# Sharing each K/V weight slab between two token groups in a fused attention and feed-forward layer

## The chip, the cores and the metric

The kernel runs on the 8 cores of one Trainium2 chip. All eight run the same program on their own inputs, with no exchange between them. The metric is the device time of the slowest core in microseconds (us).

## What is computed

One layer on an input of 2 batches x 4096 tokens x 4096 features, in float32 outside and bfloat16 inside the kernel. The reference, cut to what matters:

```python
def attn(q, w_qkv, w_dense):          # q: [2, 4096, 4096]
    qkv = q @ w_qkv.T                 # 32 query heads, 8 K and 8 V heads of 128
    ...
    scores = einsum('bskgd,btkd->bkgst', qh, kh) * scale   # causal
    probs = softmax(where(causal, scores, min))
    return einsum('bkgst,btkd->bskgd', probs, vh).reshape(...) @ w_dense.T

def ffn(x, w12, b12, w3, b3):
    x1, x2 = split(x @ w12.T + b12)   # 4096 each
    return (silu(x1) * x2) @ w3.T + b3

x = x + layernorm(attn(layernorm(x)))
x = x + layernorm(ffn(layernorm(x)))
```

## The kernel before

A core owns 8 blocks of 128 tokens of one batch, for which it computes the output, and it computes K and V for all 32 blocks of that batch itself. Weights come as a tape of slabs in the order of use: a slab holds the 4096 x 128 weights of one output chunk, in float32 in memory (2 MB), cast to bfloat16 while it is loaded.

The program goes through these stages:

1. **K and V (loop over `grp`, 8 groups of 4 blocks).** `prep_block` (four times per group) loads a block (`xscr<-xb`, L304), takes the layernorm statistics on DVE (L218, L223) and ACT (L227, L231), normalizes (L239), and transposes the block in four batches of eight 128 x 128 transposes on PE (L248), each copied out by DVE (L253) into one of the two slots of `xnT2`. Then come 16 output chunks, 8 of K and 8 of V. A chunk is `proj_ochunk`: 32 matmuls of 128 x 512 (L281), which consume one slab. ACT evicts the chunk into `kstage` (L335) or `vstage` (L344). A K chunk is stored at once. A V chunk is transposed on PE right behind its own matmuls (L248, four transposes that wait for ACT's eviction), copied by DVE into `vtstage` and stored.
2. **Q.** Eight `prep_block` for the core's own blocks fill both slots of `xnT2`; then 32 slabs, each used for both slots (`gi` 0 and 1): 64 chunks, evicted by ACT into `qstage` (L377).
3. **Attention**, then the output projection (`pp<-attn`), then the residual, two layernorms and the transposes into `xn2T` for the 8 own blocks (loop over `tb`).
4. **Feed-forward.** 32 times: a slab for `x1` and one for `x2` on both halves of the tokens (`th`, 512 tokens each), SiLU and product; then `w3`, the last layernorm and the store.

The order on every engine is the order in which the code emits operations: each of the five engines replays its own list. So the preparation of a group stands on PE and DVE behind all chunks of the group before it, the V transposes included.

**The slab ring.** `wsl` has 3 slots, each for half a slab (`load_half`, issued by POOL at L204). Half n goes into slot n % 3 and waits until the last matmul that reads half n-3 is done:

```python
    def load_half():
        n = half_loaded[0]
        slot = n % 3
        waits = [half_done[n - 3]] if (n - 3) in half_done else []
```

`half_done` is written by `proj_ochunk`, so where a slab is used by two calls, the second call sets it. In stages 2 to 4 a slab serves two calls; in stage 1 it serves one. The whole K/V weight set therefore stands 8 times on the tape. The loads of the next group's blocks stand in POOL's list behind all half-slab loads of this group.

Of the kernel before, what the change touches and what calls it, by code (L numbers as in the profile page):

```python
# [12 lines left out]
AF = mybir.ActivationFunctionType  # L13
# [21 lines left out]
TB = 128  # L35
GA1 = 4
EXP_SHIFT = -25.0

def derived(cfg):
    d = dict(cfg)  # L40
    d["D"] = cfg["IC"] * 128
    d["S"] = cfg["NBLK"] * TB
    d["TPC"] = cfg["NOWN"] * TB
    d["M"] = cfg["MC"] * 128
    d["QOC"] = cfg["KVH"] * cfg["G"]
    assert d["QOC"] == cfg["IC"]
    d["KVOC"] = 2 * cfg["KVH"]
    d["NG1"] = cfg["NBLK"] // GA1
    d["OWNG"] = cfg["NOWN"] // 2
    d["NA2T"] = d["OWNG"] * TB  # L50
    assert d["NA2T"] <= 512
    d["NSLAB_A1"] = d["NG1"] * d["KVOC"]
    d["NSLAB"] = (d["NSLAB_A1"] + d["QOC"] + cfg["IC"] + 2 * cfg["MC"] + cfg["IC"])
    pads = []
    for m in range(cfg["NOWN"] // 2):
        pads.append(2 * R * m + R)
        pads.append(2 * R * m + 2 * R)
    d["PADS"] = pads
    return d
# [45 lines left out]
def build(cfg):  # L105
    d = derived(cfg)
    IC, KVH, G, NBLK, NOWN, MC = (cfg[k] for k in ("IC", "KVH", "G", "NBLK", "NOWN", "MC"))
    D, S, TPC, M, QOC, KVOC = (d[k] for k in ("D", "S", "TPC", "M", "QOC", "KVOC"))
# [182 lines left out]
    def sdma(sem, dst_ap, src_ap, waits):  # L291
        p.op("sync", lambda sy, dst_ap=dst_ap, src_ap=src_ap: sy.dma_start(dst_ap, src_ap),
             waits=waits, inc=sem, incn=16)
        return (sem, p.v(sem))
# [22 lines left out]
        return ev  # L317

    pb = 0
    for grp in range(NG1):  # L320
        evs = []
        for j in range(GA1):
            blk = grp * GA1 + j
            evs.append(prep_block(xbt[blk], pb % 2, grp % 2, j * 128,
                                  is_first=(grp == 0 and j == 0)))
            pb += 1
        xn_ok = ("vEV", evs[-1])
        for o in range(KVOC):
# [5 lines left out]
            if o < KVH:
                p.op("scalar", lambda s, bank=bank, par=par: s.activation(  # L335
                    kstage[:, par, :], pp[:, bank, :], AF.Copy),
                    waits=[("mPE", mm), WAR.get(("kst", par), ("aR", 0))], inc="aEV")
                bank_free[bank] = ("aEV", p.v("aEV"))
                sv = sdma(f"dSK{par}", KDR[o][:, grp * 512:(grp + 1) * 512],
                          kstage[:, par, :], [("aEV", p.v("aEV"))])  # L340
                WAR[("kst", par)] = sv
            else:
                kv = o - KVH
                p.op("scalar", lambda s, bank=bank, par=par: s.activation(  # L344
                    vstage[:, par, :], pp[:, bank, :], AF.Copy),
                    waits=[("mPE", mm), WAR.get(("vst", par), ("mTR", 0))], inc="aEV")
                bank_free[bank] = ("aEV", p.v("aEV"))
                aev = p.v("aEV")
                ev = transpose_batch(
                    lambda j, par=par: vstage[:, par, 128 * j:128 * (j + 1)],  # L350
                    4, vtstage[:, par, :, :],
                    first_waits=[("aEV", aev)],
                    dst_war=[WAR.get(("vts", par), ("aR", 0))])
                WAR[("vst", par)] = ("mTR", p.v("mTR"))
                sv = sdma(f"dSV{par}",
                          VDR[kv, grp * GA1:(grp + 1) * GA1].rearrange("b t d -> t b d"),
                          vtstage[:, par, :, :], [("vEV", ev)])
                WAR[("vts", par)] = sv
        WAR[("xnT", grp % 2)] = ("mPE", p.v("mPE"))

    A1_K = [("dSK0", p.v("dSK0")), ("dSK1", p.v("dSK1"))]
    A1_V = [("dSV0", p.v("dSV0")), ("dSV1", p.v("dSV1"))]
# [163 lines left out]
    C_MM = p.v("mPE")  # L526
    C_EV = p.v("vEV")

    for tb in range(NOWN):
        par = tb % 2  # L530
        w0 = [("mPE", C_MM)] if tb < 2 else [WAR.get(("xstr", par), ("vLN", 0))]
        p.op("gpsimd", lambda g, tb=tb, par=par: g.dma_start(xstrip[:, par, :], xow[tb]),
             waits=w0, inc=f"dX{par}", incn=16)
        dx = (f"dX{par}", p.v(f"dX{par}"))
        ar = ln_stats(ytm[:, tb, :], par, first_waits=[("vEV", C_EV)])
        x2w = WAR.get(("x2s", par), ("aR", 0))
        p.op("vector", lambda v, tb=tb, par=par: v.tensor_scalar(
            x2stage[:, par, :], ytm[:, tb, :], mvt[:, par, 0:1], rst[:, par, 0:1],
            ALU.subtract, ALU.mult),
            waits=[("aR", ar), x2w] + ([("mTR", A_TR_DONE)] if tb < 2 else []), inc="vLN")  # L540
        vv = p.v("vLN")
        p.op("vector", lambda v, par=par: v.tensor_tensor(
            x2stage[:, par, :], x2stage[:, par, :], xstrip[:, par, :], ALU.add),
            waits=[("vLN", vv), dx], inc="vLN")
        vv2 = p.v("vLN")
        sv = sdma(f"dSX{par}", X2DR[tb], x2stage[:, par, :], [("vLN", vv2)])
        WAR[("x2s", par)] = sv
        ar3 = ln_stats(x2stage[:, par, :], par, first_waits=[("vLN", vv2)])
        nv = ln_norm(xstrip[:, par, :], x2stage[:, par, :], par, ar3)
        dst_war = ([("mIT", B_IT), ("vAT", B_AT), ("vMS", B_MS)] if tb == 0 else ())  # L550
        transpose_strip(
            xstrip[:, par, :], IC,
            lambda ic0, n, tb=tb: xn2T[:, ic0:ic0 + n, tb * 128:(tb + 1) * 128],
            src_ready=("vLN", nv), dst_war=dst_war)
        WAR[("xstr", par)] = ("mTR", p.v("mTR"))
    XN2T_OK = ("vEV", p.v("vEV"))
    X2_ST = [("dSX0", p.v("dSX0")), ("dSX1", p.v("dSX1"))]

    for m in range(MC):
        h1 = load_slab()  # L560
        mm1 = {}
        mm2 = {}
        for th in range(NTH):
            extra = [XN2T_OK] if (m == 0 and th == 0) else []
            mm1[th] = proj_ochunk(th % 2, lambda i, th=th: xn2T[:, i, th * THW:(th + 1) * THW],
                                  h1, extra=extra, nw=THW)
        h2 = load_slab()
        for th in range(NTH):
            mm2[th] = proj_ochunk(2 + th % 2, lambda i, th=th: xn2T[:, i, th * THW:(th + 1) * THW],
                                  h2, nw=THW)  # L570
        for th in range(NTH):
            par = th % 2
            p.op("scalar", lambda s, th=th, par=par, m=m: s.activation(  # L573
                silst[:, par, 0:THW], pp[:, th % 2, 0:THW], AF.Silu, bias=bsb[:, m:m + 1]),
                waits=[("mPE", mm1[th]), WAR.get(("sil", par), ("vLN", 0))], inc="aEV")
            bank_free[th % 2] = ("aEV", p.v("aEV"))
            aev = p.v("aEV")
            x4w = ([("mPE", C_MM), ("mTR", p.v("mTR"))] + X2_ST) if (m == 0 and th == 0) else []
            p.op("vector", lambda v, th=th, par=par, m=m: v.scalar_tensor_tensor(  # L579
                x4[:, m, th * THW:(th + 1) * THW], pp[:, 2 + th % 2, 0:THW], bsb[:, MC + m:MC + m + 1],  # L580
                silst[:, par, 0:THW], ALU.add, ALU.mult),
                waits=[("mPE", mm2[th]), ("aEV", aev)] + x4w, inc="vLN")
            bank_free[2 + th % 2] = ("vLN", p.v("vLN"))
            WAR[("sil", par)] = ("vLN", p.v("vLN"))
# [77 lines left out]
def make_tape(cfg, w_qkv, w_dense, w12, w3):  # L662
    d = derived(cfg)
    IC, KVH, MC = cfg["IC"], cfg["KVH"], cfg["MC"]
    D, M = d["D"], d["M"]

    def slabs(W):
        O = W.shape[0]
        W4 = W.reshape(O // 128, 128, IC, 128)
        return np.ascontiguousarray(W4.transpose(0, 3, 2, 1))  # L670

    wq = w_qkv[0:D]
    wk = w_qkv[D:D + KVH * 128]
    wv = w_qkv[D + KVH * 128:D + 2 * KVH * 128]
    kv_slabs = np.concatenate([slabs(wk), slabs(wv)], axis=0)
    s1 = slabs(w12[0:M])
    s2 = slabs(w12[M:2 * M])
    inter = np.empty((2 * MC, 128, IC, 128), dtype=w12.dtype)
    inter[0::2] = s1
    inter[1::2] = s2  # L680
    tape = np.concatenate([np.concatenate([kv_slabs] * d["NG1"], axis=0),
                           slabs(wq), slabs(w_dense), inter, slabs(w3)], axis=0)
    assert tape.shape[0] == d["NSLAB"]
    return np.ascontiguousarray(tape)
# [75 lines left out]
```

How the kernel before makes its waits and increments, by code:

```python
    def replay(self, eng, obj):  # L90
        for fn, waits, inc, incn in self.ops[eng]:
            for s, v in waits:
                obj.wait_ge(self.sems[s], v)
            ins = fn(obj)
            if inc is not None:
                ins.then_inc(self.sems[inc], incn)
```

## Time and profile before

| | |
|---|---|
| time of the two runs shown | 5386.72 and 5641.98 us, median 5514.35 us |
| the profiled execution: its own time | 5381.83 us |
| its span, slowest core | 5380.3 us |
| spans of the eight cores | 5357.6 to 5380.3 us |
| mean granted TensorE clock, each core | 0.908 to 0.910 |
| half-slab loads | 576 of 512 KB (as bfloat16) |
| HBM read | 771.87 MB |

The profile is of one execution on its slowest core. "Granted clock" is the share of TensorE's full clock (2.4 GHz) that the chip let through. Busy time of an engine is summed over its instructions; idle time is put down to what ended it. A PE row's duration of one matmul (about 380 ns) is longer than the distance between two, since matmuls are pipelined; the distances are read from start times.

### The profile page before, as it was taken

How to read it: one execution, taken by the hardware profiler on the slowest of the kernel's cores; microseconds unless marked ns; L12 is line 12 of the kernel's file. 1: busy time of each engine (PE TensorE's matmuls, PEld its weight loads, DVE VectorE, ACT ScalarE, POOL GpSimd, SP SyncE). 2: the span in 40 equal slices, each digit the busy share in tenths (PEclk: the TensorE clock that was granted, in tenths of full speed). 3: DMA queues.
4: the chain of work that ended last, by engine and by line, in shares of the span. 5: the costliest groups of instructions: out<-in, count | busy, mean ns of one | idle time of the engine just before them, and what ended most of it. 6: DMA issues, size and time to landing. Idle time of an engine off the chain costs nothing.

```text
span 5380.3 us, 55151 instructions; the slowest of 8 cores (5357.6 to 5380.3 us)
## 1 busy us (share of the span) xinstructions
PE 4209.1 (78%) x20096; PEld 1903.7 (35%) x20096; DVE 1144.8 (21%) x1552; ACT 975.8 (18%) x1603; POOL 331.3 (6%) x631
## 2 busy tenths in 40 slices
PE   5586587678666998888888888871699999988880
PEld 2233233333233443333333333331344444433330
DVE  2202211221223000443333300016300000011116
ACT  0000000000000000778888600000000000000000
POOL 0010011011000000000000000000000000000000
PEclk9797798788787999999999999995799999999995
DMA  6786686686673555222222133343344444433334
GB/s 100 117 139 108 103 147 114 107 142 115 107 121 71 94 96 114 65 65 60 74 62 58 33 64 65 65 71 78 75 79 75 75 79 77 72 63 63 63 59 187
DMA packets 222943, 473.46 MB, mean 88 GB/s; under 512 B 81328, under 2 KB 138672, under 8 KB 212448
## 3 DMA queue, kind: packets, MB, share of 16 engines
q0 software_dynamic: 89952, 352.48, 40.1%
q1 hardware_dynamic: 132736, 117.46, 7.3%
q8 instruction: 175, 2.87, 0.2%
q14 instruction: 80, 0.66, 0.1%
HBM read 771.87 MB, written 50.33 MB: 153 GB/s over the span
## 4 chain that ended last, share of the span: by engine, by line
PE 63%; DVE 13%; ACT 10%; DMA 7%; issue 6%; ACTq 0%; DVEq 0%; SPq 0%; POOL 0%; POOLq 0%
PE pp L281 54%; ACT psl L417 8%; DVE stats L218 5%; PE pt L248 5%; DMA wsl<-wtape 4%; PE pp L465 2%; DVE xnT L253 2%; DMA xscr<-xb 1%; PE pp L471 1%; DMA xstrip<-X2DR 1%; PE pp L409 1%; DVE xnscr L239 1%; DVE psl L456 1%; DVE lntmp L481 1%; DVE ydst L595 1%
## 5 line engine op out<-in xcount | busy, mean ns | idle before, releaser
L281 PE MATMUL pp<-xnT,wsl 128*128 128x512 bf16 x6144 | 1367.1, 382 | 39.3 <-DMA wsl<-wtape 23.0
L281 PE MATMUL pp<-xn2T,wsl 128*128 128x512 bf16 x4096 | 887.7, 380 | 3.0 <-DMA wsl<-wtape 2.0
L281 PEld LDWEIGHTS pp<-xnT,wsl 128*128 128x128 bf16 x6144 | 594.1, 98 | 791.2 <-issue 111.9
L417 ACT ACTIVATE psl<-pp,bsb 128x512 bf16<-128x512 f32 x1152 | 743.3, 687 | 194.0 <-PE pp L409 190.4
L281 PEld LDWEIGHTS pp<-xn2T,wsl 128*128 128x128 bf16 x4096 | 401.4, 98 | 489.2 <-issue 8.3
L204 POOL DMA_DIRECT2D wsl<-wtape x576 | 304.1, 529 | 4350.3 <-PE pp L281 4301.6
L465 PE MATMUL pp<-psl,vsl 128*128 128x512 bf16 x1152 | 442.6, 384 | 125.4 <-DVE psl L456 79.8
L248 PE MATMUL pt<-idsb,xnscr 128*128 128x128 bf16 x1280 | 162.0, 307 | 479.0 <-DVE xnscr L239 363.6
L281 PE MATMUL pp<-attn,wsl 128*128 128x512 bf16 x2048 | 454.5, 380 | 4.9 <-DVE attn L486 4.5
L281 PE MATMUL pp<-x,wsl 128*128 128x512 bf16 x2048 | 452.3, 379 | 1.1 <-DVE x L579 1.1
L471 PE MATMUL pp<-psl,onesb 128*128 128x512 bf16 x1152 | 443.4, 385 | 0.0
L409 PE MATMUL pp<-qsl,ksl 128*128 128x512 bf16 x1152 | 418.8, 382 | 14.6 <-DMA qsl<-QDR 14.6
L456 DVE TENSOR_TENSOR psl<-psl,msl 128x512 bf16<-128x512 bf16 x256 | 107.1, 424 | 960.3 <-ACT psl L417 494.5
L248 PEld LDWEIGHTS pt<-idsb,xnscr 128*128 128x128 bf16 x1280 | 124.0, 139 | 515.9 <-issue 515.9
L281 PEld LDWEIGHTS pp<-attn,wsl 128*128 128x128 bf16 x2048 | 196.3, 98 | 233.8 <-issue 8.6
L281 PEld LDWEIGHTS pp<-x,wsl 128*128 128x128 bf16 x2048 | 195.7, 98 | 228.7 <-issue 1.5
L465 PEld LDWEIGHTS pp<-psl,vsl 128*128 128x128 bf16 x1152 | 111.2, 97 | 386.6 <-issue 373.6
L253 DVE COPY vtstage<-pt 128x512 bf16<-128x512 bf16 x64 | 27.2, 425 | 1014.8 <-PE pt L248 1014.8
L481 DVE RECIPROCAL lntmp<-pp 128x512 f32<-128x512 f32 x64 | 214.9, 3358 | 60.8 <-PE pp L471 60.8
L579 DVE SCALAR_TENSOR_TENSOR x<-pp,bsb,silst 128x512 bf16<-128x512 f32 x64 | 48.1, 751 | 842.8 <-PE pp L281 842.8
L218 DVE BATCH_NORM_STATS2 stats<-xscr 128x6 f32<-128x512 bf16 x320 | 193.4, 677 | 21.1 <-DMA xscr<-xb 21.1
L573 ACT ACTIVATE silst<-pp,bsb 128x512 bf16<-128x512 f32 x64 | 44.0, 687 | 822.9 <-PE pp L281 822.9
(40 smaller groups left out, 1178.0 us busy)
## 6 DMA issues: line engine op xcount, KB each, us to landing
wsl<-wtape POOLq DMA_DIRECT2D x576, 512.0 KB, 6.0
xscr<-xb POOLq DMA_DIRECT2D x32, 1024.0 KB, 10.7
msl<-mtab SPq DMA_DIRECT2D x64, 512.0 KB, 3.6
yout<-ostage SPq DMA_DIRECT2D x8, 2048.0 KB, 7.9
KDR<-kstage SPq DMA_DIRECT2D x64, 128.0 KB, 6.7
VDR<-vtstage SPq DMA_DIRECT2D x64, 128.0 KB, 5.9
xscr<-xown POOLq DMA_DIRECT2D x8, 1024.0 KB, 8.0
QDR<-qstage SPq DMA_DIRECT2D x64, 128.0 KB, 4.5
```

The lines of the kernel that those rows point to most:

```text
L204: p.op("gpsimd", lambda g, n=n, slot=slot: g.dma_start(wsl[:, slot, :, :], wtape[n // 2][:, (n % 2) * IC2:(n % 2 + 1) * IC2, :]), waits=wa ...
L218: p.op("vector", lambda v, k=k, par=par, in_ap=in_ap: v.bn_stats(stats[:, par, 6 * k:6 * k + 6], in_ap[:, 512 * k:512 * (k + 1)]), waits=( ...
L239: p.op("vector", lambda v, out_ap=out_ap, in_ap=in_ap, par=par: v.tensor_scalar(out_ap, in_ap, mvt[:, par, 0:1], rst[:, par, 0:1], ALU.sub ...
L248: p.op("tensor", lambda t, j=j, tiles_fn=tiles_fn: t.transpose(pt[:, j, :], tiles_fn(j), idsb), waits=(list(first_waits) + [pt_free[0]] if ...
L253: p.op("vector", lambda v, dst_ap=dst_ap, n=n: v.tensor_copy(dst_ap, pt[:, 0:n, :]), waits=[("mTR", tr)] + list(dst_war), inc="vEV")
L281: p.op("tensor", lambda t, i=i, bank=bank, hs=hs, rhs_fn=rhs_fn, nw=nw: t.matmul(pp[:, bank, 0:nw], wsl[:, hs, i % IC2, :], rhs_fn(i), sta ...
L409: p.op("tensor", lambda t_, sbank=sbank, slot=slot, qslot=qslot, tt=t: t_.matmul(pp[:, sbank, :], ksl[:, slot, tt, :], qsl[:, qslot].rearr ...
L417: p.op("scalar", lambda s, sbank=sbank, sl3=i % 3: s.activation(psl[:, sl3, :], pp[:, sbank, :], AF.Exp, bias=bsb[:, SHIFT_COL:SHIFT_COL + ...
L456: p.op("vector", lambda v, sl3=sl3, qslot=qslot, w=w: v.tensor_tensor(psl[:, sl3, :], psl[:, sl3, :], msl[:, qslot, w, :], ALU.mult), wait ...
L465: st=(t == 0), sp=(t == pad - 1): t_.matmul(pp[:, pb, :], vsl[:, slot, tt, :], psl[:, sl3, :], start=st, stop=sp, skip_group_check=True),
L471: st=(t == 0), sp=(t == pad - 1): t_.matmul(pp[:, ob, :], onesb, psl[:, sl3, :], start=st, stop=sp, skip_group_check=True),
L481: p.op("vector", lambda v, par=par: v.reciprocal(lntmp[:, par, :], pp[:, ONB[par], :]), waits=[("mIT", itv), lnt_war[par]], inc="vAT")
```

## The change

The loop over 8 groups becomes a loop over 4 pairs of groups. A pair first prepares its 8 blocks, 4 into each slot of `xnT2`; then every K/V slab is loaded once and used for both groups (`gi` 0 and 1). The tape holds the K/V weights 4 times. The PSUM bank of a chunk is now `(2 * o + gi) % 4` and the staging buffer is `gi`; both still alternate from chunk to chunk as before. Both slots of `xnT2` are free for the next pair once the last matmul of the pair is done.

In the feed-forward stage the first matmul no longer waits for the transposes of all own blocks, but for those of its own half of the tokens; the first matmul of the other half has a wait of its own.

```diff
-    d["NSLAB_A1"] = d["NG1"] * d["KVOC"]
+    d["NSLAB_A1"] = (d["NG1"] // 2) * d["KVOC"]
...
-    for grp in range(NG1):
-        evs = []
-        for j in range(GA1):
-            blk = grp * GA1 + j
-            evs.append(prep_block(xbt[blk], pb % 2, grp % 2, j * 128,
-                                  is_first=(grp == 0 and j == 0)))
-            pb += 1
-        xn_ok = ("vEV", evs[-1])
+    for pair in range(NG1 // 2):
+        xn_ok = {}
+        for gi in range(2):
+            grp = 2 * pair + gi
+            evs = []
+            for j in range(GA1):
+                blk = grp * GA1 + j
+                evs.append(prep_block(xbt[blk], pb % 2, gi, j * 128,
+                                      is_first=(pair == 0 and gi == 0 and j == 0)))
+                pb += 1
+            xn_ok[gi] = ("vEV", evs[-1])
         for o in range(KVOC):
             halves = load_slab()
-            bank = o % 4
-            mm = proj_ochunk(bank, lambda i, g2=grp % 2: xnT2[:, g2, i, 0:512],
-                             halves, extra=[xn_ok], nw=512)
-            par = (grp * KVOC + o) % 2
...
+            for gi in range(2):
+                grp = 2 * pair + gi
+                bank = (2 * o + gi) % 4
+                mm = proj_ochunk(bank, lambda i, gi=gi: xnT2[:, gi, i, 0:512],
+                                 halves, extra=[xn_ok[gi]], nw=512)
+                par = gi
...
-        WAR[("xnT", grp % 2)] = ("mPE", p.v("mPE"))
+        WAR[("xnT", 0)] = ("mPE", p.v("mPE"))
+        WAR[("xnT", 1)] = ("mPE", p.v("mPE"))
...
+        th_of = (tb + 1) * TB // THW - 1 if ((tb + 1) * TB) % THW == 0 else None
+        if th_of is not None:
+            XN2T_TH[th_of] = ("vEV", p.v("vEV"))
...
-            extra = [XN2T_OK] if (m == 0 and th == 0) else []
+            extra = [XN2T_TH[th]] if m == 0 else []
...
-    tape = np.concatenate([np.concatenate([kv_slabs] * d["NG1"], axis=0),
+    tape = np.concatenate([np.concatenate([kv_slabs] * (d["NG1"] // 2), axis=0),
```

The body of the chunk (eviction, V transposes, stores) is the same, one level deeper.

On POOL, from the program's start, the loads of blocks (`xscr`) and of half slabs (`wsl`) change so:

```order
-L304 DMA xscr<-xb 128x4096 x4
+L304 DMA xscr<-xb 128x4096 x8
 L204 DMA wsl<-wtape 128x2048 x32
-L304 DMA xscr<-xb 128x4096 x4
+L304 DMA xscr<-xb 128x4096 x8
 L204 DMA wsl<-wtape 128x2048 x32
```

Each run of 32 half slabs now serves 8 blocks of tokens, and there are 4 such runs where there were 8.

On PE, where a group ends and the next begins, before: the last V chunk (32 matmuls) and its transposes (`vstage`), the 128 transposes of the next group's preparation (`xnscr`), its 8 K chunks and first V chunk in a row (288 matmuls), and the first V transposes.

```order
L281 MATMUL pp<-xnT_50,wsl 128x512 x32
L248 MATMUL pt<-idsb,vstage 128x128 x4
L248 MATMUL pt<-idsb,xnscr 128x128 x128
L281 MATMUL pp<-xnT_50,wsl 128x512 x288
L248 MATMUL pt<-idsb,vstage 128x128 x4
```

The same place after, between the first pair and the second:

```order
L281 MATMUL pp<-xnT_50,wsl 128x512 x32
L248 MATMUL pt<-idsb,vstage 128x128 x4
L248 MATMUL pt<-idsb,xnscr 128x128 x256
L281 MATMUL pp<-xnT_50,wsl 128x512 x544
L248 MATMUL pt<-idsb,vstage 128x128 x4
```

The preparation is now of 8 blocks, and 544 matmuls (16 K chunks and the first V chunk) follow it; there are 4 such places with the Q stage's where there were 8, and the V transposes keep their place behind each V chunk.

At the start of the feed-forward stage on PE (`xstrip` are the transposes of the last own block; `vEV` counts DVE's copies out of the transposes, `dW` the slab loads), before:

```order
L248 MATMUL pt<-idsb,xstrip 128x128 x7
L281 MATMUL pp<-xn2T,wsl 128x512 [waits dW0,aEV,vEV]
L281 MATMUL pp<-xn2T,wsl 128x512 x15
L281 MATMUL pp<-xn2T,wsl 128x512 [waits dW1]
L281 MATMUL pp<-xn2T,wsl 128x512 x15
L281 MATMUL pp<-xn2T,wsl 128x512 [waits dW0,aEV]
```

And after:

```order
L248 MATMUL pt<-idsb,xstrip 128x128 x7
L281 MATMUL pp<-xn2T,wsl 128x512 [waits dW1,aEV,vEV]
L281 MATMUL pp<-xn2T,wsl 128x512 x15
L281 MATMUL pp<-xn2T,wsl 128x512 [waits dW2]
L281 MATMUL pp<-xn2T,wsl 128x512 x15
L281 MATMUL pp<-xn2T,wsl 128x512 [waits dW1,aEV,vEV]
```

The first feed-forward matmul still stands behind all transposes of all 8 own blocks in PE's list. What changed is the count of `vEV` that it waits for, the added wait of the other half of the tokens, and the ring slots (the number of half slabs before this stage has changed).

## Rows read from the trace of the kernel before

**Rows 1.** page: granted clock in 40 slices, chain that ended last

```profile
PEclk9797798788787999999999999995799999999995
...
PE 63%; DVE 13%; ACT 10%; DMA 7%; issue 6%; ACTq 0%; DVEq 0%; SPq 0%; POOL 0%; POOLq 0%
PE pp L281 54%; ACT psl L417 8%; DVE stats L218 5%; PE pt L248 5%; DMA wsl<-wtape 4%; PE pp L465 2%; DVE xnT L253 2%; DMA xscr<-xb 1%; PE pp L471 1%; DMA xstrip<-X2DR 1%; PE pp L409 1%; DVE xnscr L239 1%; DVE psl L456 1%; DVE lntmp L481 1%; DVE ydst L595 1%
```

**Rows 2.** timeline of ACT: start us, us, op; evictions of projected chunks

```profile
88.32 0.60 ACT L335 ACTIVATE kstage<-pp 128x512 bf16<-128x512 f32 x1 [18.46 <-PE pp L281]
95.23 0.60 ACT L335 ACTIVATE kstage<-pp 128x512 bf16<-128x512 f32 x1 [6.31 <-PE pp L281]
...
147.58 0.60 ACT L344 ACTIVATE vstage<-pp 128x512 bf16<-128x512 f32 x1 [6.90 <-PE pp L281]
...
197.98 0.60 ACT L344 ACTIVATE vstage<-pp 128x512 bf16<-128x512 f32 x1 [7.81 <-PE pp L281]
206.38 0.60 ACT L344 ACTIVATE vstage<-pp 128x512 bf16<-128x512 f32 x1 [7.81 <-PE pp L281]
279.62 0.60 ACT L335 ACTIVATE kstage<-pp 128x512 bf16<-128x512 f32 x1 [18.24 <-PE pp L281]
...
398.62 0.60 ACT L344 ACTIVATE vstage<-pp 128x512 bf16<-128x512 f32 x1 [7.97 <-PE pp L281]
473.74 0.60 ACT L335 ACTIVATE kstage<-pp 128x512 bf16<-128x512 f32 x1 [18.75 <-PE pp L281]
...
1438.66 0.60 ACT L335 ACTIVATE kstage<-pp 128x512 bf16<-128x512 f32 x1 [19.78 <-PE pp L281]
...
1499.53 0.60 ACT L344 ACTIVATE vstage<-pp 128x512 bf16<-128x512 f32 x1 [6.52 <-PE pp L281]
...
1559.08 0.60 ACT L344 ACTIVATE vstage<-pp 128x512 bf16<-128x512 f32 x1 [7.96 <-PE pp L281]
1695.10 0.60 ACT L377 ACTIVATE qstage<-pp 128x512 bf16<-128x512 f32 x1 [19.38 <-PE pp L281]
...
1806.92 0.60 ACT L377 ACTIVATE qstage<-pp 128x512 bf16<-128x512 f32 x1 [6.31 <-PE pp L281]
```

**Rows 3.** windows: K chunks, preparation of four blocks, Q, feed-forward

```profile
core 0: us, PE busy (x) PEld busy (x) DVE busy (x) ACT busy (x) POOL busy (x), PEclk, DMA share, GB/s
79.60:148.40 68.80, 64.81 (x288) 27.97 (x288) 0.00 (x0) 5.38 (x9) 9.35 (x18) 1.00 0.87 141
...
209.00:271.00 62.00, 16.21 (x129) 12.44 (x130) 37.03 (x56) 1.99 (x8) 2.64 (x5) 0.50 0.45 77
...
1685.50:1807.00 121.50, 120.53 (x546) 53.88 (x547) 0.00 (x0) 9.63 (x17) 8.45 (x16) 0.98 0.48 87
...
3821.00:4712.00 891.00, 887.87 (x4099) 401.48 (x4098) 48.07 (x64) 45.28 (x65) 67.54 (x128) 1.00 0.45 75
```

**Rows 4.** line L281 in 80:1560: what its matmuls waited for

```profile
  DMA wsl<-wtape: 19.5, 36
...
  ACT kstage L335: 4.5, 5
```

**Rows 5.** line L281 in 1685:2141 (Q)

```profile
  DMA wsl<-wtape: 3.5, 4
```

**Rows 6.** timeline, end of first group, and of the last

```profile
195.43 1.07 POOL L304 DMA_DIRECT2D xscr<-xb  x2
...
209.03 4.85 DVE L218 BATCH_NORM_STATS2 stats<-xscr 128x6 f32<-128x512 bf16 x8 [0.81 <-DMA xscr<-xb]
...
1560.83 4.84 DVE L218 BATCH_NORM_STATS2 stats<-xscr 128x6 f32<-128x512 bf16 x8
```

**Rows 7.** slab issues of 80:148, then of 1685:1807: count, KB, us to landing

```profile
wsl<-wtape POOLq DMA_DIRECT2D x17, 512.0 KB, 6.5
...
wsl<-wtape POOLq DMA_DIRECT2D x16, 512.0 KB, 6.3
```

**Rows 8.** timeline, start of the feed-forward matmuls

```profile
3820.66 19.59 PE L281 MATMUL pp<-xn2T,wsl 128*128 128x512 bf16 x83 [0.94 <-DVE xn2T L253]
```

More of the change, by code:

```diff
@@ L319, in build @@
     pb = 0
-    for grp in range(NG1):
-        evs = []
-        for j in range(GA1):
-            blk = grp * GA1 + j
-            evs.append(prep_block(xbt[blk], pb % 2, grp % 2, j * 128,
-                                  is_first=(grp == 0 and j == 0)))
-            pb += 1
-        xn_ok = ("vEV", evs[-1])
+    assert NG1 % 2 == 0
+    for pair in range(NG1 // 2):
[9 more added lines that the diff above has]
+            xn_ok[gi] = ("vEV", evs[-1])
@@ L328, in build @@
         for o in range(KVOC):
             halves = load_slab()
-            bank = o % 4
-            mm = proj_ochunk(bank, lambda i, g2=grp % 2: xnT2[:, g2, i, 0:512],
-                             halves, extra=[xn_ok], nw=512)
-            par = (grp * KVOC + o) % 2
[L334 to L358, printed above, removed]
@@ L359, in build @@
-        WAR[("xnT", grp % 2)] = ("mPE", p.v("mPE"))
+            for gi in range(2):
[4 more added lines that the diff above has]
+                par = gi
+                if o < KVH:
+                    p.op("scalar", lambda s, bank=bank, par=par: s.activation(
+                        kstage[:, par, :], pp[:, bank, :], AF.Copy),
+                        waits=[("mPE", mm), WAR.get(("kst", par), ("aR", 0))], inc="aEV")
+                    bank_free[bank] = ("aEV", p.v("aEV"))
+                    sv = sdma(f"dSK{par}", KDR[o][:, grp * 512:(grp + 1) * 512],
+                              kstage[:, par, :], [("aEV", p.v("aEV"))])
+                    WAR[("kst", par)] = sv
+                else:
+                    kv = o - KVH
+                    p.op("scalar", lambda s, bank=bank, par=par: s.activation(
+                        vstage[:, par, :], pp[:, bank, :], AF.Copy),
+                        waits=[("mPE", mm), WAR.get(("vst", par), ("mTR", 0))], inc="aEV")
+                    bank_free[bank] = ("aEV", p.v("aEV"))
+                    aev = p.v("aEV")
+                    ev = transpose_batch(
+                        lambda j, par=par: vstage[:, par, 128 * j:128 * (j + 1)],
+                        4, vtstage[:, par, :, :],
+                        first_waits=[("aEV", aev)],
+                        dst_war=[WAR.get(("vts", par), ("aR", 0))])
+                    WAR[("vst", par)] = ("mTR", p.v("mTR"))
+                    sv = sdma(f"dSV{par}",
+                              VDR[kv, grp * GA1:(grp + 1) * GA1].rearrange("b t d -> t b d"),
+                              vtstage[:, par, :, :], [("vEV", ev)])
+                    WAR[("vts", par)] = sv
@@ L527, in build @@
     C_EV = p.v("vEV")
+    XN2T_TH = {}
     for tb in range(NOWN):
```

## The prediction

> **What bounds the kernel now.** I read the chain of waits first, then where each projected chunk is evicted, then each stage's windows. The chain [rows 1] runs through PE for 63% of the span, and the largest line is the projection's, L281, at 54%; slab loads are only 4% of it, DVE 13%. So the kernel is a queue of matmuls with holes, and the change can win only what lies in holes of the K/V stage: about 256 of the 576 half-slab loads are in that stage, and halving them is worth nothing by itself. The granted clock [rows 1] dips in the slices that hold preparations of token blocks; those are the big holes, and the change removes none of them: 40 blocks are prepared before and after.
>
> The evictions [rows 2] give the stage's timetable, since there is one behind each chunk. From the first K chunk (88.32) to the first Q chunk (1695.10) it lasts 1606.8 us. I split it in three:
> - Eight K parts (first K to first V eviction, 8 intervals each). The first takes 147.58 - 88.32 = 59.3 us, the last 1499.53 - 1438.66 = 60.9; all eight sum to 478.5. The shortest interval is 95.23 - 88.32 = 6.91 us, 32 matmuls with no gap; 64 of these are 442.2. The 36.3 us above that are waits for slabs, with the time in which PE's pipeline runs empty and fills.
> - Eight V parts (first to last V eviction, 7 intervals): the first 206.38 - 147.58 = 58.8, the last 1559.08 - 1499.53 = 59.6, the sum 473.6. One interval is 206.38 - 197.98 = 8.40 to 8.41; the 1.5 us more than a K chunk are the eviction and the four transposes behind it, which stand in PE's list.
> - Seven restarts from a last V to the next first K eviction, with four blocks prepared between: 73.24 for the first, 75.12 for the second (the longest), 518.6 in all; and the one into Q, with eight blocks: 1695.10 - 1559.08 = 136.02.
>
> Is the K part really short of slabs? In the K window PE is at full clock with DMA busy 0.87; in Q, where a slab serves two chunks, DMA is at 0.48 [rows 3]. Over the K/V stage the matmuls of L281 sat 19.5 us in 36 waits for `wsl` and 4.5 in five put down to ACT's `kstage`, whose bank had long been free, so I count these as slabs too [rows 4]. In Q, half as many chunks, it is 3.5 us in four [rows 5]. The landing times explain it only in part, 6.5 us in K against 6.3 in Q [rows 7]. The ring does the rest. A half slab is issued when the slot three halves back is done, and is needed two halves, 6.9 us, later: 6.5 plus the issue makes every half a near miss. With reuse only one half in two has that deadline (the second half of a slab, issued when the other group has used the first half of the slab before), and it comes once in 13.8 us; the other half gets twice the time.
>
> **The change part by part.** The Q stage already runs the order that the K/V stage gets: eight blocks prepared, then each slab used twice. So I price by its rows.
> - *K parts.* Four of 16 intervals. Q's first 16 take 1806.92 - 1695.10 = 111.8 us, its own waits of 1.3 included. 4 x 111.8 = 447.3, against 478.5: -31.3. Bounds: no wait at all, 442.2 (-36.3); or every interval keeps the 0.57 us it loses now (36.3 / 64), which is no gain (0), if landing time rather than the ring should be the limit. I take Q, the nearest row; K chunks store 128 KB each as Q chunks do.
> - *V parts.* The transposes are not halved: 64 V chunks remain, each with its own. Four parts of 15 intervals at 8.41: 504.6, against 473.6: +31.0, because four former restarts are now plain V intervals. Bounds: 60 at the last part's mean of 8.51 would be 510.5 (+6 on this), none below 8.41.
> - *Restarts.* Before the first K eviction four more blocks are prepared; four blocks take 62.0 [rows 3], so 88.32 + 62.0 = 150.3. Then four restarts of the eight-block kind: 4 x 136.02 = 544.1. Together 694.4, against 88.32 + 518.6 + 136.02 = 742.9: -48.5. With the four V intervals taken off, a dropped restart is worth only 3.7 us: DVE, ACT and PE work through a block in series whether it is the first or the fifth. What goes is the way from a group's last V chunk to the next statistics and the first matmuls at half clock (0.50 is granted during a preparation [rows 3]). Bounds: the seven restarts differ by 2 us, so four by 4 us either way.
> - *Block loads.* The first two of the next pair stand in POOL's list behind the last half slab. That is issued 13.6 us before the statistics start, which wait 0.8 us for them [rows 6]. In a pair it is issued about 7 us earlier (the last slab serves two chunks), so this wait should go; at the step into Q statistics already start with no wait on a load (the row at 1560.83 has none [rows 6]). It is in the 136.02.
> - *Wait for both `xnT2` slots.* It holds only DVE copies whose transposes stand in PE's list behind the same matmuls. Nothing queues behind it that could run: 0.
> - *First feed-forward matmul.* It stands behind all transposes in PE's list, so the looser count can save no more than the wait for DVE's last copy, 0.94 us [rows 8]; the added wait of the other half of the tokens comes 32 matmuls later and is long met. -0.9, bounds -0.9 and 0.
>
> Sum: -31.3 + 31.0 - 48.5 - 0.9 = -49.7 us. The profiled execution took 5381.83 us, so 5332, or -0.9%. Everything behind Q's first chunk keeps its length. The lower of the two timed runs, 5386.72, is within 0.1% of the profiled one; the median of 5514.35 is the middle of that and of one at 5641.98, which no row explains. I forecast an execution like the profiled one.
>
> Worst ends together: 0 for K, +6 for V, +4 for restarts leave -49.7 + 31.3 + 10 + 0.9 = -7.5, 5374. Best ends: -49.7 - 5 - 4 = -58.7, 5323. Executions of one kernel may differ by a few tenths of a per cent more.
>
> **The rivals.**
> - *Landing time is the limit (no gain in K).* A tight half still has 6.9 us, and 6.3 is not far from 6.5. For: the four waits in Q have a mean of 0.9 us, longer than K's 0.5 [rows 4, 5]. Against: they are only four in 32 slabs, where K and V have 41 in 128. Time: 5381.8 - 49.7 + 31.3 = 5363. Halfway, 5348.
> - *The clock turns it slower.* A pair idles PE at half clock for 124 us instead of 62, then wants 32 chunks in a row. If full clock came back late, each chunk at half clock would take 6.9 us more (the clock's two levels, 1.2 and 2.4 GHz). It decides at 49.7 / 6.9 = 7 chunks over the stage, nearly two behind each restart; at six behind each, 24 x 6.9 = 166 us, 5498, slower by 2.2%. For: 0.50 in the preparation. Against: Q restarts from the same eight blocks and its window of 121.5 us has 0.98 granted; 891 us of feed-forward have 1.00 [rows 3].
> - By the Trainium skill (TensorE: Matmul & The Clock Gate, the warning on the peak-current limiter) three busy cores of a die take it to 13/16 of the clock in dense matmuls, and the denser K part might be what trips it; as an estimate from that page 128 chunks would then take 1.6 us more each, +204 us, 5536. The trace disagrees: the K window, with all eight cores at work, has 1.00 [rows 3]; I give this rule 1 of the 4 in 100 below.
> - *The change doesn't do what it says.* If the second use of a slab did not hold its slot, there would be a race and not a time; the slot's release is the later of the two calls. POOL's list has half the loads. What is left is that the slabs were hidden anyway: that is the first rival.
> - *More than 2% faster.* That takes 108 us; waits for slabs (36.3), V's excess (2.7) and restarts do not add up to it. Preparation would have to get shorter too, and its 62.0 us for four blocks [rows 3] are the same work of DVE, ACT and PE in series.
>
> **How the numbers follow.** The forecast (5323 to 5345) has 0.72, the K part keeping much of its waits (5346 to 5375) 0.18, a kernel slower by the clock 0.04, more than 59 us won 0.06. Within the first, 5332 is the likeliest. The range, 5308 to 5380, adds some 15 us of scatter below and takes in the first rival above. A measurement of this kernel tells about 2% from no change. Faster by over 2%: 0.03; within 2%: 0.94; slower by over 2%: 0.03.
>
> **What would show it.** Right: 448 half-slab loads; K/V stage with four blocks of 16 K intervals of 6.9 to 7.1 us; V intervals still 8.4; restarts near 136 and the first Q eviction near 1646 us; DMA share in K near 0.5; L281's waits for `wsl` in the stage below 8 us in some 20. Wrong: K intervals still at 7.5, the first Q eviction at 1677 (first rival); granted clock under 0.9 in K windows (second); a restart much unlike 136, or V intervals of 9 us, would mean that a store or a copy has become late, which I see no row for.

## The result, and the profile after

| | before | changed |
|---|---|---|
| lowest time | 5374.23 us | 5316.31 us |
| median of all runs | 5731.78 us (10 runs) | 5516.49 us (11 runs) |
| ratio | | 0.9886, 95% interval 0.9867 to 0.9905 |

The change makes the kernel 1.1% faster (0.95 to 1.3%), about 61 of 5381 us; that is "within 2%". In many executions (7 of the 10 and 7 of the 11 above, 4 of 6 of e6) the cores of one die or of both had a lower granted clock, which lifts the medians; the ratios, and the times given as measured for the experiments, are of the other executions. Spans and mean granted clocks by core in the profiled execution:

```profile
core 0: 5318.2 us, clock 0.914
...
core 5: 5728.1 us, clock 0.837
...
die 0 (median of its cores): 5312.6 us, clock 0.915
die 1 (median of its cores): 5698.8 us, clock 0.840
```

Cores 0 to 3 were granted 0.914 to 0.916 (the kernel before had 0.908 to 0.910), so I read the changed kernel on core 0, with its span of 5318.2 us. The page below is of a second profiled execution of the same kernel (the run e5 below). Granted clock in 40 slices, HBM traffic, and the chain that ended last, by engine and by line:

```profile
PEclk9995986977968999999999999985899999999995
...
HBM read 637.65 MB, written 50.33 MB: 129 GB/s over the span
...
PE 67%; DVE 13%; ACT 10%; issue 6%; DMA 3%; ACTq 0%; DVEq 0%; SPq 0%; POOL 0%; POOLq 0%
PE pp L281 58%; ACT psl L424 8%; DVE stats L218 5%; PE pt L248 5%; PE pp L472 2%; DVE xnT L253 2%; PE pp L478 1%; DMA xstrip<-X2DR 1%; PE pp L416 1%; DVE xnscr L239 1%; DVE psl L463 1%; DVE lntmp L488 1%; DVE ydst L606 1%; DMA wsl<-wtape 1%; ACT ydst L522 1%
```

Against [rows 1], PE's share of the chain goes from 63 to 67% and the slab loads' from 4 to 1%: the chain is the same one with holes taken out. HBM reads fall from 771.87 to 637.65 MB, which is the 64 slabs of 2 MB. The dips of the clock at the start are fewer and wider.

The changed kernel's timetable on core 0 of the first profile, the answer to [rows 2]. Timeline of ACT, evictions of chunks: first and second K of the first pair, its first and last V, first K of the second pair, last V of the fourth pair, first Q:

```profile
147.97 0.60 ACT L341 ACTIVATE kstage<-pp 128x512 bf16<-128x512 f32 x1 [16.92 <-PE pp L281]
154.88 0.60 ACT L341 ACTIVATE kstage<-pp 128x512 bf16<-128x512 f32 x1 [6.31 <-PE pp L281]
...
258.48 0.60 ACT L350 ACTIVATE vstage<-pp 128x512 bf16<-128x512 f32 x1 [6.25 <-PE pp L281]
...
384.88 0.60 ACT L350 ACTIVATE vstage<-pp 128x512 bf16<-128x512 f32 x1 [7.97 <-PE pp L281]
...
519.36 0.60 ACT L341 ACTIVATE kstage<-pp 128x512 bf16<-128x512 f32 x1 [17.75 <-PE pp L281]
...
1498.13 0.60 ACT L350 ACTIVATE vstage<-pp 128x512 bf16<-128x512 f32 x1 [7.97 <-PE pp L281]
...
1634.49 0.60 ACT L384 ACTIVATE qstage<-pp 128x512 bf16<-128x512 f32 x1 [19.74 <-PE pp L281]
```

One K part of 16 intervals takes 258.48 - 147.97 = 110.5 us, 6.91 each, with no time lost; the V part of 15 intervals 126.4; the restart to the second pair 134.48, the one into Q 136.36. The first Q eviction is at 1634.5 where it was at 1695.1.

The same core's K window (columns as in [rows 3]; DMA share is the last but one number), then what the matmuls of L281 waited for over the whole stage (the answer to [rows 4]), and the slab issues of this window (to [rows 7]):

```profile
core 0: us, PE busy (x) PEld busy (x) DVE busy (x) ACT busy (x) POOL busy (x), PEclk, DMA share, GB/s
150.00:255.00 105.00, 105.00 (x489) 47.57 (x487) 0.00 (x0) 8.96 (x15) 8.44 (x16) 1.00 0.50 94
```

```profile
  DMA wsl<-wtape: 1.1, 1
```

```profile
wsl<-wtape POOLq DMA_DIRECT2D x16, 512.0 KB, 5.9
```

PE is busy for the whole window and the DMA share is 0.50 where it was 0.87. Over the whole stage one wait of 1.1 us for a slab is left of 36. The landing time, 5.9 us, is 0.6 below the former 6.5.

The end of the first pair, as in [rows 6]: last half slab, first two block loads, first statistics:

```profile
364.81 0.53 POOL L204 DMA_DIRECT2D wsl<-wtape  x1 [12.91 <-PE pp L281]
365.33 1.06 POOL L304 DMA_DIRECT2D xscr<-xb  x2
...
386.63 4.84 DVE L218 BATCH_NORM_STATS2 stats<-xscr 128x6 f32<-128x512 bf16 x8
```

The block loads start 21.3 us ahead of the statistics (13.6 before), and the statistics no longer wait for them.

### The profile page after: what moved, and what is told of

Read it like the earlier page. It is cut to its first block, busy times and chain, and to the rows that moved or that the text cites. A ratio compares the mean times of both kernels' runs of the same rounds, so it can differ in the third digit from the quotient of the medians.

```text
span 5728.1 us, 54896 instructions; the slowest of 8 cores (5306.7 to 5728.1 us)
## 1 busy us (share of the span) xinstructions
PE 4608.7 (80%) x20096; PEld 2006.2 (35%) x20096; DVE 1144.6 (20%) x1552; ACT 983.8 (17%) x1603; POOL 263.7 (5%) x503
## 3 DMA queue, kind: packets, MB, share of 16 engines
HBM read 637.65 MB, written 50.33 MB: 120 GB/s over the span
## 4 chain that ended last, share of the span: by engine, by line
PE 72%; DVE 12%; ACT 8%; issue 5%; DMA 2%; ACTq 0%; DVEq 0%; SPq 0%; POOL 0%; POOLq 0%
PE pp L281 60%; ACT psl L424 6%; PE pt L248 5%; DVE stats L218 5%; PE pp L472 3%; PE pp L478 2%; PE pp L416 2%; DVE xnT L253 2%; DMA xstrip<-X2DR 1%; DVE xnscr L239 1%; DVE psl L463 1%; DVE ydst L606 1%; DVE lntmp L488 1%; ACT vstage L350 1%; ACT ydst L522 1%
## 5 line engine op out<-in xcount | busy, mean ns | idle before, releaser
L281 PE MATMUL pp<-xnT,wsl 128*128 128x512 bf16 x6144 | 1348.1, 381 | 3.0 <-DMA wsl<-wtape 2.0
L281 PE MATMUL pp<-xn2T,wsl 128*128 128x512 bf16 x4096 | 1076.1, 437 | 1.3 <-DMA wsl<-wtape 1.3
L281 PEld LDWEIGHTS pp<-xnT,wsl 128*128 128x128 bf16 x6144 | 598.8, 98 | 728.7 <-issue 21.8
L281 PEld LDWEIGHTS pp<-xn2T,wsl 128*128 128x128 bf16 x4096 | 445.5, 109 | 631.4 <-issue 630.2
L281 PE MATMUL pp<-attn,wsl 128*128 128x512 bf16 x2048 | 550.1, 437 | 4.7 <-DVE attn L493 4.5
L281 PE MATMUL pp<-x,wsl 128*128 128x512 bf16 x2048 | 548.7, 436 | 1.1 <-DVE x L590 1.1
L478 PE MATMUL pp<-psl,onesb 128*128 128x512 bf16 x1152 | 458.8, 398 | 0.0
L204 POOL DMA_DIRECT2D wsl<-wtape x448 | 236.4, 528 | 4632.2 <-PE pp L281 4575.7
L416 PE MATMUL pp<-qsl,ksl 128*128 128x512 bf16 x1152 | 435.0, 396 | 17.2 <-DMA qsl<-QDR 17.2
L281 PEld LDWEIGHTS pp<-attn,wsl 128*128 128x128 bf16 x2048 | 219.0, 108 | 301.8 <-issue 301.7
L281 PEld LDWEIGHTS pp<-x,wsl 128*128 128x128 bf16 x2048 | 218.7, 108 | 297.1 <-issue 296.9
```

The source lines that it names most:

```text
L204: p.op("gpsimd", lambda g, n=n, slot=slot: g.dma_start(wsl[:, slot, :, :], wtape[n // 2][:, (n % 2) * IC2:(n % 2 + 1) * IC2, :]), waits=wa ...
L281: p.op("tensor", lambda t, i=i, bank=bank, hs=hs, rhs_fn=rhs_fn, nw=nw: t.matmul(pp[:, bank, 0:nw], wsl[:, hs, i % IC2, :], rhs_fn(i), sta ...
L416: p.op("tensor", lambda t_, sbank=sbank, slot=slot, qslot=qslot, tt=t: t_.matmul(pp[:, sbank, :], ksl[:, slot, tt, :], qsl[:, qslot].rearr ...
L478: st=(t == 0), sp=(t == pad - 1): t_.matmul(pp[:, ob, :], onesb, psl[:, sl3, :], start=st, stop=sp, skip_group_check=True),
```

## The experiments

The numbers by stage are from the timeline of ACT in each profiled execution. "K" is the sum of all K parts of a core (64 intervals) and "between" the sum of the three restarts between pairs; where no core is named they are means over the eight cores. Runs e1 to e4 were on one chip, e5 to e7 on another.

**e5, the changed kernel again**, on the chip of e6 and e7.

> The changed kernel once more, on the chip of the next two. The undone waits of the run before cost 5.7 us up to the first Q eviction there; if that is right the changed kernel has its first Q eviction at 1633 to 1637 us on all cores, restarts of 133 to 135 us, and a whole of 5315 to 5325. If the 10 us between the two kernels' dies were a matter of the chip, it comes out 4 or more higher.

Measured: 5317.1 to 5323.5 us, ratio 0.9887 (0.987 to 0.9904). The first Q eviction came at 1631 to 1641 us by core (mean 1634.6), where 1633 to 1637 was expected. The first K eviction was at 148.2 (146.3 to 150.3 by core), between was 401.9, the restart into Q 135.5 and K 443.6. Single restarts took 133.0 to 134.8 us. The result repeats.

**e1, the early waits undone.**

```diff
-                                 halves, extra=[xn_ok[gi]], nw=512)
+                                 halves, extra=[xn_ok[1]], nw=512)
...
-            extra = [XN2T_TH[th]] if m == 0 else []
+            extra = [XN2T_OK] if (m == 0 and th == 0) else []
```

> The changed kernel with the two early waits undone: the first matmul of a pair waits for all eight prepared blocks, and the first feed-forward matmul for all eight own blocks; the reuse of slabs stays. Theory (the early wait in the K/V stage, which the prediction did not price, is what makes the restarts shorter than 136 us): on an undisturbed core the first K eviction comes 1.1 to 1.5 us later than 148 (149.1 to 149.5), each of the three restarts between pairs takes 134.5 to 136 us instead of 133.0 to 134.5, and the whole is 5 to 7 us longer than the changed kernel's 5316 to 5321, so 5322 to 5328. Rival (the shorter restarts are chance, the moment at which the clock comes back): restarts stay 133.0 to 134.5 and the whole stays within 2 us of the changed kernel.

Measured: 5328.4 to 5334.0 us, ratio 0.9906 (0.9877 to 0.9935). The first K eviction was at 149.5 (+1.3 against e5; by core it scatters by 4 us in both), between 406.3 (+4.4, so +1.45 for each restart), into Q 135.4 (no difference, and the edit does not touch it), K 444.5. The first theory holds. The slowest core lost 10 to 11 us, more than the 5 to 7 expected. The rest lies on two cores of this chip: cores 4 and 5 had a granted clock of 0.99 in 155:255 where the other six had 1.00, and K sums of 448.5 and 448.9 where the others had 442.3 to 444.2. The other six have a mean span of 5318.5, 6.5 us above the mean of e5's cores, and the 5.7 with the 0.9 of the feed-forward wait make 6.6. How the wait works is seen in two timelines. First the changed kernel at the start of the second pair (PE's last transposes, its first matmuls, DVE's last copy):

```profile
509.32 1.01 PE L248 MATMUL pt<-idsb,xnscr 128*128 128x128 bf16 x8 [0.95 <-DVE xnT L253]
...
510.12 10.16 PE L281 MATMUL pp<-xnT,wsl 128*128 128x512 bf16 x37
510.43 0.69 DVE L253 COPY xnT<-pt 128x1024 bf16<-128x1024 bf16 x1 [1.26 <-PE pt L248]
```

and then e1 at the same place (transposes, copy, matmuls, first K eviction):

```profile
509.72 1.01 PE L248 MATMUL pt<-idsb,xnscr 128*128 128x128 bf16 x8 [0.94 <-DVE xnT L253]
510.84 0.69 DVE L253 COPY xnT<-pt 128x1024 bf16<-128x1024 bf16 x1 [1.26 <-PE pt L248]
...
511.68 10.61 PE L281 MATMUL pp<-xnT,wsl 128*128 128x512 bf16 x39 [0.94 <-DVE xnT L253]
...
520.92 0.60 ACT L341 ACTIVATE kstage<-pp 128x512 bf16<-128x512 f32 x1 [18.91 <-PE pp L281]
```

In the changed kernel the matmuls of the first group start at 510.12, right behind the transposes of the eighth block and before its last copy: they need only the first four blocks. In e1 they wait 0.94 us for that copy, 1.96 us after the transposes' start where it was 0.80. That is 1.16 us later.

**e2, the feed-forward wait alone**, put on the kernel before (`XN2T_TH` as in the change).

> The kernel before with the feed-forward wait edit alone. Theory: the first feed-forward matmul no longer waits 0.94 us for DVE's last copy, the whole is 0.9 to 1.5 us shorter, below what timing tells; the trace shows no idle time before that matmul. Rival (it is worth several us and explains the 11 us by which the forecast of 5332 fell short of the gain): 5 us or more shorter, and the stage from the last transposes on starts earlier by that much.

Measured: ratio 0.9997 (0.9939 to 1.0054), which tells nothing at this size; the trace does. In the kernel before, L281's waits in 3700:3860 hold this row:

```profile
  DVE xn2T L253: 0.9, 1
```

In e2, and in the changed kernel, no such row is left in that stretch. So the edit takes away its 0.9 us; for several us there is no wait in this stretch that it could have taken away, and the rival falls by the trace, not by the times.

e2 has the K/V stage of the kernel before, on the chip of e4, and e4 is compared with it below. Its K sums were 462 to 468 us on cores 0 to 3 (476.4 is their mean in the profile of the kernel before), and 482.5 and 489.9 on cores 4 and 5. The K window of core 4 shows a granted clock of 0.95:

```profile
80.00:147.00 67.00, 65.17 (x271) 28.05 (x276) 0.00 (x0) 4.78 (x8) 8.81 (x17) 0.95 0.83 137
```

**e3, pairs without reuse.** Order, slots and waits of the changed kernel, but each half slab loaded again for the second group.

```diff
-            halves = load_slab()
             for gi in range(2):
+                halves = load_slab()
                 grp = 2 * pair + gi
```

> The changed kernel with every half slab loaded again for the second group of the pair (576 half slabs as before), order and waits otherwise as changed. Theory (the K part gained because only one half in two has a tight deadline): each of 16 K intervals loses about 0.57 us again, a K part of 16 takes 118 to 121 us instead of 110.5, the first Q eviction comes at 1665 to 1675 instead of 1634.5, and the whole is about 5350 (5345 to 5358). Rival (pairing itself, with half as many cold starts of the ring, brings the gain): K parts stay under 113 and the whole under 5328.

Measured: ratio 0.9978 (0.9957 to 0.9999), lowest time 5370.7 us, 13 above the upper end of what was expected. Between was 403.7, nearly as with reuse; K was 482 to 500 by core (mean 488.9), one part 118 to 133. The K window of core 0, and the waits of L281 over the whole stage:

```profile
150.00:265.00 115.00, 107.26 (x484) 45.74 (x483) 0.00 (x0) 8.96 (x15) 16.15 (x31) 1.00 0.99 156
```

```profile
  DMA wsl<-wtape: 22.4, 32
  ACT kstage L341: 5.3, 6
```

At a DMA share of 0.99 PE is busy for 107.3 of 115.0 us, and in the stage it waits 38 times instead of once. So the pairing by itself gives next to nothing, and the reuse gives the gain. In means over the cores, the pairing saves 19.7 us in restarts less V intervals and loses 14.1 in K (474.8 before, 488.9 here); the first Q eviction goes from 1688.0 to 1682.4, and with the reuse to 1634.6. A K interval lasts 7.42 us on average before, and here 7.55 in the first eight of a part and 7.73 in the last eight. That the ring catches up in V chunks, which now come half as often, would explain it; no run tests this. The theory had the sign and the mechanism; its 0.57 us for each interval was too small, core 0 lost (483.2 - 442.0) / 64 = 0.64 and core 7 0.91.

**e4, the kernel before with a fourth slot** for half slabs in the K/V stage, traffic as before.

```diff
-        slot = n % 3
-        waits = [half_done[n - 3]] if (n - 3) in half_done else []
+        slot = n % 4 if n < NH_A1 else n % 3
+        waits = [half_done[slot_last[slot]]] if slot in slot_last else []
+        slot_last[slot] = n
```

> The kernel before with a fourth half-slab slot in the K/V stage, nothing else; traffic as before. Theory (ring depth, not the rate of the DMA engines, makes the K waits): with three halves of 3.45 us instead of two to land in, the K parts fall from a mean of 59.8 to 55.3 to 56 us, and the whole by 28 to 36 us, to about 5345 to 5353. Rival (the rate: DMA busy share is 0.91 to 0.97 in the K parts, so a deeper ring only queues more): the K parts stay at 58 or more and the whole gains less than 12 us, landing times grow to 9 us.

Measured: ratio 1.0029 (1.0014 to 1.0044), not faster, but by core it is two stories. On cores 0 to 3 every K part took 55.2 to 55.3 us, 6.91 for each chunk. Evictions of the second group on core 0 (first K, first V, second V):

```profile
274.93 0.60 ACT L342 ACTIVATE kstage<-pp 128x512 bf16<-128x512 f32 x1 [18.46 <-PE pp L288]
...
330.18 0.60 ACT L351 ACTIVATE vstage<-pp 128x512 bf16<-128x512 f32 x1 [6.31 <-PE pp L288]
338.68 0.60 ACT L351 ACTIVATE vstage<-pp 128x512 bf16<-128x512 f32 x1 [7.91 <-PE pp L288]
```

The K windows of cores 0 and 4:

```profile
281.00:338.00 57.00, 55.95 (x263) 25.29 (x261) 0.42 (x1) 4.78 (x8) 8.44 (x16) 1.00 1.00 167
```

```profile
281.00:338.00 57.00, 56.66 (x242) 24.89 (x245) 0.00 (x0) 4.78 (x8) 8.45 (x16) 0.93 0.98 152
```

Core 0 keeps full clock with the DMA share at 1.00. Cores 4 and 5 have their K parts at 59 to 60, yet PE is busy for 56.66 of 57 us (core 4): it does not wait for slabs, but its granted clock is 0.93. This is not the fourth slot's doing: the same two cores had 0.95 in e2, with three slots. Nor does full DMA traffic suffice for it: in e3, with 0.99 and 1.00 on these two, their clock was 1.00 in 160:255, though PE was busy there for only 88 of 95 us.

So the first theory is right on the ring. The three slots, not the rate of the DMA engines, made K wait: K falls to 442.0 on four cores, by 32 to 37 us against the profile of the kernel before and by 20 to 26 against e2. The forecast of the whole is wrong twice. First, the restarts grew, on core 0 from a mean of 74.1 to 75.1, and in sum by 7 to 17 us on cores 0 to 3. There, the end of the third group:

```profile
393.11 0.42 DVE L260 COPY vtstage<-pt 128x512 bf16<-128x512 bf16 x1 [10.42 <-DMA VDR<-vtstage]
393.45 4.84 DVE L225 BATCH_NORM_STATS2 stats<-xscr 128x6 f32<-128x512 bf16 x8
```

The last V copy waits for the store two chunks before (`VDR<-vtstage`) and comes late, and the statistics behind it. On core 0 this happens at the end of all eight groups, and never in the kernel before. Second, the slowest core sets the time, here one with less clock. The spans of cores 0 to 3 were 5340 to 5355 in the profiled execution; their mean of 5347 stands against 5366 for the same cores of the kernel before on that chip: there the fourth slot did win some 20 us.

**e6, preparation inside the chunks.** The changed kernel with four slots of transposed blocks (two more in memory that is free in this stage); while a pair runs its 32 chunks, the next eight blocks are loaded, normalized and transposed, one batch of eight transposes in the middle of each chunk. The place of the batch in `proj_ochunk` (the rest of the edit spreads the steps of a block over four chunks):

```diff
             if i == IC2 - 1:
                 half_done[n0] = ("mPE", p.v("mPE"))
+                if hook is not None:
+                    hook()
```

> The changed kernel with the preparation of the next eight blocks spread over the 32 chunks of the running pair, one batch of eight transposes in the middle of each chunk, two more pairs of slots for the transposed blocks in memory that is free in this stage. Theory (a restart is serial work of DVE, ACT and PE that PE could spend in matmuls): four restarts of 135 us shrink to one V interval each, -505 us; 128 batches in PE's list cost 0.5 to 1.2 us each, +65 to +150; whole 4870 to 4970. Rival (DVE's 4.8 us of statistics stand ahead of the copy that frees the transposes' bank, and PE waits for it in every fourth chunk): V intervals of 10 us and more, whole 5000 or more. Rival 2 (without pauses the clock is lowered): K intervals of 8 us and more on some cores also in the best executions.

Measured: 4888.8 and 4901.3 us, ratio 0.9096 (0.9074 to 0.9118). A K interval is mostly 7.35 us (+0.44 for a batch), a V interval 8.8 to 9.3; the first Q eviction is at 1198 to 1210. Both rivals fall: of the 480 V intervals of the eight cores three reach 10.0 us, not every fourth; eight of the 512 K intervals pass 8 us, at most 8.8, but the K window 155:260 has a clock of 1.00 on every core, and the page's clock row shows no dips in the stage:

```profile
PEclk9999999999999999999999999758999999999995
```

```profile
core 0: 4877.9 us, clock 0.958
...
core 5: 4899.7 us, clock 0.957
```

The timeline of core 0 where the second pair begins, and two chunks in it:

```profile
400.16 0.60 ACT L409 ACTIVATE vstage<-pp 128x512 bf16<-128x512 f32 x1 [8.26 <-PE pp L284]
...
401.57 0.42 DVE L256 COPY vtstage<-pt 128x512 bf16<-128x512 bf16 x1 [4.22 <-PE pt L251]
...
402.14 0.61 PE L251 MATMUL pt<-idsb,xnscr 128*128 128x128 bf16 x8 [0.74 <-DVE vtstage L256]
402.86 0.69 DVE L256 COPY xnTd<-pt 128x1024 bf16<-128x1024 bf16 x1 [0.86 <-PE pt L251]
...
403.69 8.68 PE L284 MATMUL pp<-xnTc,wsl 128*128 128x512 bf16 x31 [0.94 <-DVE xnTd L256]
...
412.52 0.60 ACT L400 ACTIVATE kstage<-pp 128x512 bf16<-128x512 f32 x1 [3.00 <-PE pp L284]
...
415.66 0.61 PE L251 MATMUL pt<-idsb,xnscr 128*128 128x128 bf16 x8
...
419.87 0.60 ACT L400 ACTIVATE kstage<-pp 128x512 bf16<-128x512 f32 x1 [6.75 <-PE pp L284]
```

The batch in a chunk (415.66) takes PE 0.61 us in a row that shows no wait before it. At a pair's start it is another matter: V's copy, the transposes, their copy and the first matmuls stand in series (401.57 to 403.69), the next 31 matmuls take 8.68 us instead of 6.9, and the interval from 400.16 to 412.52 is 12.4 us. PE was busy for 1.0 of the 3.6 us from 400.0, and in 403.7:407 its granted clock was 0.50, then 1.00 again. The clock does not fall each time: of the 32 such places of the eight cores, 21 have an interval of 10.7 us, as core 2 has here with the same gap, and the other 11 have 12.0 to 13.7.

**e7, the same without reuse.**

> The same spread preparation, but every half slab loaded again for the second group of the pair. Theory (reuse is worth the slab waits only, as in the paired kernel without reuse: 0.6 to 0.7 us in a K interval): 64 K intervals give 40 us, and V intervals, which now hold a batch of transposes more but also share the DMA engines with block loads of 2 MB each, give 0 to 60; 40 to 100 us longer than the kernel with reuse. Rival (the batches in mid-chunk give the slabs the time they lacked): less than 15 us longer.

Measured: 5068.2 to 5090.9 us, ratio 0.9442 (0.9415 to 0.9468): 180 us slower than e6, nearly twice the upper end of what was expected. On core 0 about one K interval in four (14 of 64) takes 10.6 to 17.2 us, most of them 13 to 17, the others 7.35 to 9.0. The timeline of one (eviction, matmuls, next eviction):

```profile
181.77 0.60 ACT L400 ACTIVATE kstage<-pp 128x512 bf16<-128x512 f32 x1 [4.48 <-PE pp L284]
...
188.50 6.39 PE L284 MATMUL pp<-xnT,wsl 128*128 128x512 bf16 x15 [7.17 <-DMA wsl<-wtape]
...
198.94 0.60 ACT L400 ACTIVATE kstage<-pp 128x512 bf16<-128x512 f32 x1 [16.57 <-PE pp L284]
```

PE sits 7.17 us for a slab. The wait costs more than itself, which the expectation left out: the 15 matmuls behind it take 6.39 us, about twice the 0.216 us that one has at full clock, and the granted clock there is 0.55:

```profile
188.50:194.80 6.30, 6.25 (x17) 2.29 (x19) 0.00 (x0) 0.00 (x0) 0.00 (x0) 0.55 0.69 140
```

So of the 17.2 us of this interval 7.2 are the wait and about 3 the clock. The long intervals come once in four chunks, as the block loads do in POOL's list (one for eight half slabs), and I read them as slabs that land behind a block of twice their size (in 176:200 four slab loads took 9.1 us to land, their median); no run here takes the block loads away alone, so this is argued and not shown. With reuse the same block loads cost next to nothing (7.65 us for the longest K interval of e6's first pair).

## Why the prediction was right or wrong

**The range on record missed; the mechanism held but for one term.** The forecast was 5332, the range 5308 to 5380. The median of the timed runs is 5516.49 and lies outside it. The step that failed there is "I forecast an execution like the profiled one": it gave no room to executions at a lower clock. The run shown at 5641.98 was dismissed with "which no row explains"; it was 4.8% above the profiled time and should have widened the range, or been named as its condition. What the runs showed in its place: 7 of the 11 had mean granted clocks of 0.77 to 0.89 on one die or both and took 5463 to 6098 us. Why the clock is lower in them stays open; executions of the kernel before have it too (down to 0.79), so it does not take the change.

Where no core lost clock the changed kernel took 5316.3 to 5321.8 us. That is in the range, but 1 to 7 us below the lower end of the likeliest case and of my "best ends together" (5323): it is the case "more than 59 us won", to which I gave 0.06. The change of 0.92% forecast stands against 1.14% (0.95 to 1.33) measured.

By its steps, on core 0, forecast and measured:

| step | forecast | measured |
|---|---|---|
| first K eviction | 150.3 | 148.0 |
| four K parts | 447.3 | 443.3 |
| four V parts | 504.6 | 505.3 |
| three restarts and the one into Q | 544.1 | 401.6 + 136.4 = 538.0 |
| first Q eviction | 1646.3 | 1634.5 |

- *What bounds the kernel:* right. The K waits went (36 to 1), and e4 shows on four cores that they came from the ring's depth, e3 that they come back, and more, when each load serves one chunk again. The split of the gain was off: the terms for the order (-48.5 and +31.0) gave it 17.5 us and the reuse 31.3, where by the first Q eviction e3 and e5 give 5.6 and 47.8. The sum does not show it, since pairs without reuse, in which K waits more than before, are in no term.
- *K parts, priced by Q's first 16 intervals:* mis-sized by 4 us. Q's 1.3 us of waits lay in its first four slabs, and on core 0 alone so many: six of the other seven cores of the same trace had 110.6 for these 16 intervals. Three of the four K parts had none. The best end of the bound (442.2) was nearly met. The landing time was 5.9 us where I had taken Q's 6.3; no run shows why, and at nearly the same DMA share it was 6.6 in the changed kernel's own Q.
- *V parts:* right to 0.7 us. The extra V intervals do take back what the K parts give.
- *Restarts, priced by 136.02:* the term of the sum that was mis-sized most, -48.5 where the trace has -56.9 with the first eviction, and beyond its bound of 4 us. I costed the same edit, an earlier count in a wait, at -0.9 in the feed-forward stage and overlooked it in the K/V stage, where `xn_ok[gi]` lets the first group start when the eighth block is transposed but not yet copied. e1 puts 1.3 us on the first eviction and 1.45 on each of three restarts: 5.7 of the 8.4 us by which these steps were too long. The mean of the eight cores for the row that I took from core 0 is 135.7, which makes another 1.4 over four restarts. The rest is not placed. In the diff it was one index; in the Q stage, by which I priced, that edit does not exist, and there 136 was right.
- *Block loads and the wait for both slots:* as forecast. The statistics no longer wait for their loads, and no wait for a slot shows.
- *Feed-forward:* right (e2).
- *First rival, landing time is the limit:* fell. *The clock turns it slower:* not in what the ratio compares; the K window has 1.00 on core 0 of both profiles. It was no idle thought: in e2 and e4 two cores of one chip had 0.93 to 0.95 in their K windows, and in e7 a wait of 7 us was followed by matmuls at half clock.
- *More than 2% faster:* right for this change, since the preparation was left as it stood. e6 shows what it hides: another 8%, 9% with this change.

What stays open: why cores 4 and 5 of one chip had less clock than cores 0 to 3 (0.99 in e1, 0.95 in e2, 0.93 in e4, but 1.00 in e3), and the last 1 us or so of the restarts and the first eviction.

## What to carry to other kernels

A halved load is worth the waits for it, with what the clock loses behind a long one: find the deadline of each slot in the ring (6.9 us here, against 6.5 to land), and ask which loads keep it after the change. When a stage is priced by a sister stage that already runs the new order, go through the diff for every edit that the sister lacks, waits above all. And a restart in which engines take turns (135 us, four times) was nine times what this change won: moving that work between the matmuls gave another 430 us, of which 180 are lost again when the slabs are not reused (e7).

## What the hardware showed that I had not expected

With twice the traffic a half slab took hardly longer to land: 5.9 us at a DMA share of 0.50 (changed kernel) and 6.8 at 0.99 (e3). So a third half in flight (e4, 6.7 us) hid all of it on four cores even at a share of 1.00. Beside block loads it was longer (9.1 us in 176:200 of e7).

In the profiled execution of the changed kernel, core 6 had this K window (core 7 also 0.81), while cores 0 to 5 had 1.00 in the same stretch:

```profile
155.00:280.00 125.00, 125.00 (x478) 51.80 (x477) 0.00 (x0) 8.96 (x15) 8.31 (x16) 0.81 0.46 80
```

Its K intervals were 134.4 / 16 = 8.4 us instead of 6.91, a ratio of 1.22. The Trainium skill (TensorE: Matmul & The Clock Gate, the warning on the peak-current limiter) describes such a level, 13/16, and says that it holds for a whole die once three cores run dense matmuls. The level, 0.81, agrees with it. The condition does not: cores 4 and 5 of the same die had 1.00 in that window and K parts of 110.5 to 111.4 us, and in e5 core 5 had 1.00 in its K window with all eight cores at the same matmuls.
